# Coefficients of a product-key expert layer: 32 weighted columns as the stationary operand in one of four column groups, 64 one-hot columns moved

## The reference, cut to what matters

```
x = x + xattn(layernorm(x), ctx)
s1, i1 = top_k(sim[0], 16); s2, i2 = top_k(sim[1], 16)
final_scores, pk = top_k(s1[..., :, None] + s2[..., None, :], 16)
final_idx = (i1 * 64 + i2) taken at pk
hidden = gelu(einsum('btd,bthkd->bthk', x_norm, expert_down[final_idx]))
hidden = hidden * relu(final_scores)
x = x + einsum('bthk,bthkd->btd', hidden, expert_up[final_idx])
```

## Time and profile before

| | us |
|---|---|
| median of 3 runs | 1187.69 (1186.41 to 1188.65) |
| the profiled execution, its own time | 1188.53 |
| its span, first to last instruction | 1186.7 |
| PE busy | 1032.1 |
| DVE busy | 951.8 |
| POOL busy | 640.9 |
| ACT busy | 393.8 |

### The profile page before, as it was taken

The page is one execution under the profiler, slowest core; times in us unless marked ns, Lnnn a source line. Parts: engine busy times, 40 slices in busy tenths (PEclk is TensorE's granted clock), DMA queues, the critical chain, the costliest instruction groups (busy, mean ns, idle before and its releaser), DMA issues.

```text
span 1186.7 us, 28163 instructions
## 1 busy us (share of the span) xinstructions
PE 1032.1 (87%) x10088; PEld 721.1 (61%) x10088; DVE 951.8 (80%) x4847; ACT 393.8 (33%) x725; POOL 640.9 (54%) x793
## 2 busy tenths in 40 slices
PE   4779989877878676479989989999999999999998
PEld 2434434323313223367878878888888878888887
DVE  4756566989998977999999899999989999953210
ACT  2246655443544353232222222222222222222211
POOL 6340340343021215567777877878777786787511
PEclk9789999888978888679999999999999999999999
DMA  5344324131221102610000000000010000010000
GB/s 169 118 146 124 116 81 127 56 112 47 90 75 43 49 7 105 246 32 6 22 21 21 22 11 26 27 11 27 7 34 22 21 16 16 26 34 8 2 18 10
DMA packets 60347, 63.82 MB, mean 54 GB/s; under 512 B 7184, under 2 KB 56592, under 8 KB 59696
## 3 DMA queue, kind: packets, MB, share of 16 engines
q1 hardware_dynamic: 60208, 62.03, 16.6%
HBM read 42.34 MB, written 19.66 MB: 52 GB/s over the span
## 4 chain that ended last, share of the span: by engine, by line
DVE 38%; PE 36%; POOL 12%; issue 7%; DMA 2%; ACT 2%; SPq 2%; DVEq 0%; POOLq 0%; ACTq 0%
PE bank L1363 33%; POOL mem L848 5%; DVE mem L1318 5%; DVE mem L1273 4%; DVE mem L1209 3%; PE bank L1366 3%; DVE mem L1156 2%; DVE mem L1155 2%; DVE mem L1205 2%; DVE mem L1212 2%; DVE mem L1192 2%; SPq L501 2%; DVE mem L1315 2%; POOL mem L714 1%; DVE mem L1160 1%
## 5 line engine op out<-in xcount | busy, mean ns | idle before, releaser
L1363 PE MATMUL bank<-mem 128*128 128x32 bf16 (+6 forms) x9608 | 983.7, 275 | 107.0 <-DVE mem L1273 34.1
L1363 PEld LDWEIGHTS bank<-mem 128*128 128x128 bf16 (+4 forms) x9608 | 668.8, 122 | 377.0 <-issue 172.4
L848 POOL TENSOR_TENSOR mem<-mem 128x1536 bf16<-128x1536 bf16 x123 | 339.8, 2763 | 137.6 <-DVE mem L1315 137.5
L1273 DVE TENSOR_REDUCE mem<-bank 128x1 f32<-128x512 f32 x256 | 167.8, 683 | 65.7 <-PE bank L1363 64.8
L969 ACT ACTIVATE mem<-bank 128x512 f32<-128x512 f32 x256 | 148.0, 603 | 189.7 <-PE bank L1363 188.9
L1318 DVE TENSOR_TENSOR mem<-mem,bank 128x2048 bf16<-128x2048 bf16 x128 | 155.5, 1215 | 0.0
L1020 ACT COPY mem<-bank 128x512 f32<-128x512 f32 x128 | 74.9, 585 | 120.9 <-PE bank L1363 120.8
L1366 PE MATMUL bank<-mem 128*128 128x128 f32 (+3 forms) x480 | 74.6, 287 | 44.3 <-DVE mem L1073 17.6
L855 POOL TENSOR_TENSOR mem<-mem 128x512 f32<-128x512 f32 x64 | 83.2, 1299 | 50.5 <-ACT mem L1009 50.5
L1366 PEld LDWEIGHTS bank<-mem 128*128 128x128 f32 (+3 forms) x480 | 55.1, 141 | 85.0 <-issue 37.2
L714 POOL TENSOR_TENSOR mem<-mem 128x32 f32<-128x32 f32 (+5 forms) x224 | 45.6, 241 | 105.2 <-DVE mem L1164 105.2
(11 more groups left out here) (105 smaller groups left out, 785.3 us busy)
## 6 DMA issues: line engine op xcount, KB each, us to landing
mem<-parts_d SPq DMA_DIRECT2D x192, 64.0 KB, 2.2
parts_d<-mem SPq DMA_DIRECT2D x16, 384.0 KB, 2.7
mem<-in_L_ffn_expert_down SPq DMA_DIRECT2D x16, 256.0 KB, 2.9
downT_d<-mem SPq DMA_DIRECT2D x16, 256.0 KB, 3.1
mem<-downT_d SPq DMA_DIRECT2D x4, 1024.0 KB, 8.0
mem<-in_L_ffn_expert_up SPq DMA_DIRECT2D x4, 1024.0 KB, 12.2
tok_d<-mem SPq DMA_DIRECT2D x16, 160.0 KB, 1.8
mem<-tok_d SPq DMA_DIRECT2D x16, 160.0 KB, 2.4
```

Of the source, the lines that this page charges most:

```text
L848: nc.gpsimd.tensor_tensor(ow[q % 2], i0, i1, ALU.mult).then_inc(ow_rdy, 1)
L1273: nc.vector.tensor_reduce(nmx[g % 2][:, i % TB, i // TB:i // TB + 1], psum[n % 3][:, :], AX.X, ALU.max, negate=True).then_inc(s_max, 1)
L1363: return nc.tensor.matmul(o, l, r, start=first, stop=last)
```

## The change

In `coefficients` the operands change places. The 32 weighted columns `ow` of a token are loaded, and 64 of its 128 one-hot columns are moved; the result, 32 partitions by 64 columns, goes to the partitions `at` = 32 (2 e + h), where e is the token's place in its pair and h the half of the one-hot columns. So four matmuls in a row belong to four column groups, and a block has 96 matmuls.

```
                 at_least(pe, c_ev, c - 1)
-                for t in range(TK):
+                for a in range(TP):
                     for w in range(3):
-                        a, e = t // PAIR, t % PAIR
-                        last = mm(psum[2 + q % 2][:, t * JL:(t + 1) * JL], oh[q % 2][:, a, :, e], ow[q % 2][:, w, a, :, e],
-                                  w == 0, w == 2)
+                        for e in range(PAIR):
+                            for h in range(2):
+                                at = 32 * (2 * e + h)
+                                last = mm(psum[2 + q % 2][at:at + 32, a * 64:(a + 1) * 64], ow[q % 2][:, w, a, :, e],
+                                          oh[q % 2][:, a, h * 64:(h + 1) * 64, e], w == 0, w == 2)
                 last.then_inc(c_mm, 1)
```

`take_coef` copies each bank in four parts, because a token's coefficients now lie on 64 partitions:

```
-                src = psum[2 + q % 2][:, :].rearrange("p (t j) -> p j t", j=JL)
-                nc.scalar.copy(coef[1 - par][:, :, q * TK:(q + 1) * TK], src).then_inc(c_ev, 1)
+                src = psum[2 + q % 2][:, :].rearrange("p (a s j) -> p s j a", a=TP, s=2)
+                dst = coef[1 - par][:, :, q * TK:(q + 1) * TK].rearrange("p j (a e) -> p e j a", e=PAIR)
+                for e in range(PAIR):
+                    for s in range(2):
+                        i = nc.scalar.copy(dst[64 * s:64 * s + 64, e], src[64 * e:64 * e + 64, s])
+                i.then_inc(c_ev, 1)
```

The experts are numbered over the partitions in another order for this, so the tables are read as "(j p) d" in place of "(p j) d", in `load_setup` and `load_up`:

```
-                src = up.rearrange("(p j) d -> p j d", j=JL)[:, i * JQ:(i + 1) * JQ, :]
+                src = up.rearrange("(j p) d -> p j d", j=JL)[:, i * JQ:(i + 1) * JQ, :]
```

and the numbers with which the high parts are compared are written in another order, with 32 more for the low parts. POOL makes them with three iotas in place of one:

```
+            for h in range(2):
+                own = numbers[:, h * P // 2:(h + 1) * P // 2, :].rearrange("p (s k) t -> p s k t", s=2)
+                nc.gpsimd.iota(own, pattern=[[2, 2], [4, JL], [0, PAIR]], base=h, channel_multiplier=0).then_inc(iconst, 1)
+            nc.gpsimd.iota(numbers[:, P:P + JL, :], pattern=[[1, JL], [0, PAIR]], base=0, channel_multiplier=0).then_inc(iconst, 1)
```

More of the change, by code:

```diff
@@ L110, in build @@
         tokS = mem.take(5 * P // 2, BF16).rearrange("p (b c t) -> p b c t", b=BPT, c=5)
-        iota = mem.take(P * PAIR // 2, BF16).rearrange("p (c t) -> p c t", c=P)
+        iota = mem.take((P + JL) * PAIR // 2, BF16).rearrange("p (c t) -> p c t", c=P + JL)
         mark = mem.at
@@ L512, in load_setup @@
                         wait_taken(sp, "down", n - 2)
-                    src = down.rearrange("(p j) d -> p j d", j=JL)
+                    src = down.rearrange("(j p) d -> p j d", j=JL)
                     sp.dma_start(dn_sb[n % 2], src[:, 2 * n:2 * n + 2, :]).then_inc(dn_ld[n % 2], 16)
@@ L805, in _ @@
                 split_projection(0, n)
-            numbers = p_sb[2].rearrange("p h t -> p (h t)")[:, 0:P * PAIR].bitcast(I32).rearrange("p (c t) -> p c t", c=P)
-            nc.gpsimd.iota(numbers, pattern=[[1, P], [0, PAIR]], base=0, channel_multiplier=0).then_inc(iconst, 1)
-            pool.wait_ge(iconst, 1)
+            numbers = p_sb[2].rearrange("p h t -> p (h t)")[:, 0:(P + JL) * PAIR].bitcast(I32)\
+                             .rearrange("p (c t) -> p c t", c=P + JL)
+            for h in range(2):
+                own = numbers[:, h * P // 2:(h + 1) * P // 2, :].rearrange("p (s k) t -> p s k t", s=2)
+                nc.gpsimd.iota(own, pattern=[[2, 2], [4, JL], [0, PAIR]], base=h, channel_multiplier=0).then_inc(iconst, 1)
+            nc.gpsimd.iota(numbers[:, P:P + JL, :], pattern=[[1, JL], [0, PAIR]], base=0, channel_multiplier=0).then_inc(iconst, 1)
+            pool.wait_ge(iconst, 3)
             nc.gpsimd.tensor_copy(iota, numbers).then_inc(iconst, 1)
@@ L967, in probabilities @@
                 if quad == 2 and hh == 0:
-                    act.wait_ge(iconst, 2)
+                    act.wait_ge(iconst, 4)
                 nc.scalar.activation(p_sb[quad % 3][:, hh, :], psum[3 + n % 2][:, :], ACT.Exp, scale=DK ** -0.5)\
@@ L1298, in end @@
                     choose_experts(LAST, *TASKS[FH + q - 1])
-            dve.wait_ge(iconst, 2)
+            dve.wait_ge(iconst, 4)
             dve.wait_ge(o_ev, NG)
-            nc.vector.tensor_copy(psum[5][:, 0:P], iota.rearrange("p c t -> p (c t)").bitcast(F32)).then_inc(iconst, 1)
-            dve.wait_ge(iconst, 3)
-            numbers = psum[5][:, 0:P].bitcast(BF16).rearrange("p (c t) -> p c t", c=P)
+            nc.vector.tensor_copy(psum[5][:, 0:P + JL], iota.rearrange("p c t -> p (c t)").bitcast(F32)).then_inc(iconst, 1)
+            dve.wait_ge(iconst, 5)
+            numbers = psum[5][:, 0:P + JL].bitcast(BF16).rearrange("p (c t) -> p c t", c=P + JL)
             def one_hots(k, par, kk, q):
@@ L1315, in one_hots @@
                 nc.vector.tensor_tensor(oj[q % 2], low.to_broadcast([P, TP, JL, PAIR]),
-                                        numbers[:, 0:JL, :].unsqueeze(1).to_broadcast([P, TP, JL, PAIR]),
+                                        numbers[:, P:P + JL, :].unsqueeze(1).to_broadcast([P, TP, JL, PAIR]),
                                         ALU.is_equal).then_inc(oh_rdy, 1)
                 nc.vector.tensor_tensor(oh[q % 2], high.to_broadcast([P, TP, P, PAIR]),
-                                        numbers.unsqueeze(1).to_broadcast([P, TP, P, PAIR]),
+                                        numbers[:, 0:P, :].unsqueeze(1).to_broadcast([P, TP, P, PAIR]),
                                         ALU.is_equal).then_inc(oh_rdy, 1)
```

## The result

The changed kernel takes 1191.09 us (median of 16 runs, 1187.89 to 1194.32). The kernel before takes 1187.39 us beside it (16 runs, 1184.67 to 1192.19). The ratio is 1.0031, 95% interval 1.0018 to 1.0044: slower by 2 to 5 us, where I had forecast 4 us faster. The time lies inside the range of the prediction, on the other side of no change.

What follows compares the result with a forecast made beforehand. DVE was taken to bound slots -1 to 5, PE slot 6: 4.6 us saved there, less 0.7 for ACT's longer copy, plus 0.2 in slots 0 to 5, gave -4.1 us, a median of 1183.6 us; range 1179 to 1206.

Steps and rivals of the forecast that it cites:

- The bound: DVE sets the pace in slots -1 to 5, PE in slot 6; of PE's saving in slots 0 to 5 0.2 us counts.
- The visit: PE's work in coefficients for one q: 0.91 us instead of 1.20, so 0.29 saved at 2.4 GHz.
- the round: Four pairs to four column groups on PE take 28 ns; 24 rounds make 0.67 us of a visit.
- A: Rival: a pair costs 25 ns wherever it lands, a visit 2.64 us, the whole 1327 us; chance 7%.
- B: Rival: a group's load and matmul take turns, 55 ns a round, a visit 1.56 us, the whole 1206 us; chance 13%.
- Slot -1: nothing, DVE sets it: In slot -1 a visit grows to 1.5 us at 1.2 GHz, under 27 us of idle PE, costing nothing.
- Cost 0.7 us; in slots 1 to 5 it falls into PE's spare time: ACT's four copies take 1.30 us, so PE waits 1.9 us for the output copy in slot 6 instead of 1.2.
- The rest: One-hots, the copy to bank 5, POOL's two more iotas and expert tables read in 1 KB rows cost nothing.
- The sum: Over the whole kernel: slot 6 saves 4.6 us less 0.7, slots 0 to 5 save 0.2, together -4.1 us.
- C: Rival: rounds of 33 to 45 ns, longer drain or fresh waits in slots 0 to 5; 1186 to 1190 us; chance 15%.

Runs made afterwards that it cites:

- e6: The changed kernel with expert weights for the next slots loaded after slot -1 and the output copied ahead of the coefficients: 1185.22 us.
- e3: The kernel before, with each of a visit's 48 pairs in slot -1 cut in two of 16 moved columns: 1192.81 us.
- e1: The changed kernel with the old shape and one copy in slot -1 alone: 1189.11 us.
- e2: The changed kernel with five of six 1 MB expert-weight loads moved, one to the end of slot -1, four into slot 0: 1189.3 us.
- e4: The kernel before with each copy of a bank of coefficients cut in four of 64x256: 1193.59 us.
- e9: The kernel before with up and down read in the changed kernel's order of rows: 1186.63 us.

## Why the prediction was wrong

- **The bound**: right. PE's saving came through in slot 6 almost alone. In slots 0 to 5 PE's busy time fell from 504.0 to 494.1 us and the stretch by 0.8, where 0.2 was forecast. The busy time fell by 9.9 only, where 96 visits at 0.20 are 19: the granted clock stood at its lower level for 22 us of these slots instead of 7 (behind slot 0's start in four short stretches, at 568, 708, 804 and 974 us, instead of one), and PE's work takes longer there (e6's 3.4 us made a step 1.7 longer). The stretch didn't become longer by it.
- **The visit**: right in kind, mis-sized. I had 0.67 + 0.24 = 0.91 us, 0.29 saved. Its loads after:

```profile
1058.27 0.85 PEld L1371 LDWEIGHTS bank<-mem 128*32 128x32 bf16 x96 [0.33 <-issue]
```

  Less one load's 0.10 that is 0.75 us over 95 distances, 7.9 ns each, 32 ns for a round of four instead of 28. Between single starts in the trace, first to last matmul takes 0.762 us, and the neighbours on both sides stand 0.093 and 0.102 us further off than before: the change of shape costs 0.195 us, where I had 0.24. With the last matmul's own distance the visit costs 0.98 us, and with the next full-width pair, which stands 0.02 us further off from its neighbour than before, 1.00: that is the 0.20 by which the step became shorter. The term that failed is the round; rivals A (25 ns a pair) and B (55 ns a round) fell. The 0.42 ns a column was read from pairs with 32 columns at 1.2 GHz, but e3's pairs with 16 columns take the same 26.7 ns, so that row didn't show the price of a column.
- **"Slot -1: nothing, DVE sets it"**: the step that failed. It weighed PE's busy time against the slot and found "27 us of idle PE". The idle time was there, but instructions didn't come in it fast enough. The sum had no term for PE's instructions, which doubled in every visit, and of the six 1 MB loads in this slot it counted four. e1 puts the whole +4.8 us on this slot, e2 shows the loads' part in it.
- **"Cost 0.7 us; in slots 1 to 5 it falls into PE's spare time"**: near enough in the changed kernel, 0.8 in slot 6. Copies took 1.53 us and not 1.30, since four stand one behind the other at 0.38 where I had read 0.33 from pairs. As a statement on slots 1 to 5 it was wrong: e4 shows 3.3 us there when the visit isn't shorter as well, 1.0 of it by the wait alone.
- **The rest**: right. e9 shows nothing for the rows.
- **The sum**: -3.9 forecast for slot 6, -2.0 found (sixteen visits brought 2.8 us, not 4.6, and the wait took 0.8). -0.2 for slots 0 to 5, -0.8 found. 0 for slot -1, +4.8 found, and this turns the sign. That is +2.0 of the +3.7 us between the medians. The other 1.7 is open: 0.9 was seen ahead of slot -1 in the one profile, in a stage that varies by 8 us, and the interval reaches down to 2.1.
- **The rivals**: C came closest, with "fresh waits in slots 0 to 5". The waits came one slot earlier and were larger.

## What to carry to other kernels

Count instructions, not only microseconds, when an edit splits work into smaller pieces: divide the instructions of the busiest short stretch by 256 and set the distance against what instruction traffic shows there, above all where large loads run in the same stretch. The sign in a trace is idle time that ends with "issue" at equal distances in instructions, in the midst of a group. And when an operation gets longer on an engine that has time, look at what stands behind it in that engine's order; here turning two calls round was worth 2 us in the kernel before, and with it turned in both kernels the change brought nothing.

## What the runs showed of the hardware that I had not expected

- PE's program text comes by the same DMA engines as data, in packets of 16 KB for some 256 instructions. While the 1 MB loads ran a packet came every 6.6 us; behind them every 3.7 to 4.2 (506.05, 509.74, 513.91, 517.67 and 521.42 us in the changed kernel). Even that is too slow for 96 pairs a visit at VectorE's shortest steps of 1.46 us, which is most likely what slot -1's last 2 us in e2 are. PE resumed 2.3 to 2.6 us after each packet began. The Trainium skill, page "Runtime: NRT & Kernel Launch", section "Instruction fetch mechanics", gives blocks of 16 KiB or 256 instructions, and the trace agrees (256 of PE's an added packet, stalls 256 apart). The same section calls the cost of crossing a block "mostly hidden"; in slot -1 of the changed kernel it isn't, with idle times of 1.2 to 4.7 us at each block.
- Pairs that go to four column groups in turn follow each other every 7.9 ns, 96 of them in a row and all with a full 128-row contraction, where pairs of full width took 25.1. Going from the full width to column groups and back cost 0.195 us a visit.
- At the 1.2 GHz level a pair of full width takes 26.7 ns for 16 columns (e3) and for 32 (before) alike: half the columns save nothing.
- Copies of 64x256 on ACT take 379 ns each and don't overlap, the same 379 as copies of 128x256: fewer partitions save nothing, and half the elements still take 65% of the 585 ns of one of 128x512.
